# The down product ahead of the next tile's transposes in a routed expert stage

## The reference

```
y = mask * (conv(u * mask, kernel) + u * mask * D)      # (32, 64, 1024)
probs = softmax(y @ gate_w.T)                            # 2048 x 16
w = top 2 of probs, divided by their sum
h = silu(y @ g.T) * (y @ u.T)                            # per expert 112 values
out = x + sum over experts of w * (h @ d.T)
```

## Time and profile before

| | |
|---|---|
| median of 3 runs | 552.07 us (548.31 to 552.22) |
| the profiled execution | 552.11 us, span 550.1 us |
| mean granted TensorE clock | 0.983 |
| TensorE matmuls, weight loads busy | 468.8 us (85%), 404.8 us (74%) |
| VectorE, ScalarE, GpSimd busy | 229.8, 102.7, 182.1 us |
| chain that ended last | TensorE 47%, DMA 32%, VectorE 9%, issue 7% |
| indirect DMAs | 42 gathers, 40 write-backs |
| expert stage, first product to last write-back issued | 268.2 to 540.0 us |

### The profile page before, as it was taken

How to read it: one execution, slowest core, us unless ns; L and a number is a source line. 1 busy time by engine, 2 the same in 40 slices (tenths; PEclk the granted TensorE clock), 3 DMA queues, 4 the chain that set the end, 5 groups by cost and what they waited for, 6 DMA issues and landing times.

```text
span 550.1 us, 9315 instructions
## 1 busy us (share of the span) xinstructions
PE 468.8 (85%) x2835; PEld 404.8 (74%) x2836; DVE 229.8 (42%) x613; ACT 102.7 (19%) x184; POOL 182.1 (33%) x215
## 2 busy tenths in 40 slices
PE   0079899998999999978689999899999899999881
PEld 0079799998999999967567767676666666777660
DVE  7987444445455421585322323233323332333321
ACT  2031111111111101120122222222222222222220
POOL 6355213222222200025233344342442543244431
PEclk9999999999999999997899999999999999999996
DMA  8757999999989987210358789889889778967653
GB/s 287 229 178 246 292 324 334 326 294 310 337 278 345 332 297 234 77 39 1 113 119 225 216 234 265 215 174 294 226 202 263 202 211 193 268 121 167 102 85 62
DMA packets 47783, 119.83 MB, mean 218 GB/s; under 512 B 7698, under 2 KB 24210, under 8 KB 47634
## 3 DMA queue, kind: packets, MB, share of 16 engines
q1 hardware_dynamic: 19314, 73.42, 39.0%
q0 software_dynamic: 11808, 37.76, 31.0%
q10 hardware_dynamic: 16640, 8.39, 5.3%
HBM read 94.62 MB, written 38.57 MB: 242 GB/s over the span
## 4 chain that ended last, share of the span: by engine, by line
PE 47%; DMA 32%; DVE 9%; issue 7%; POOL 3%; POOLq 1%; ACT 0%; DVEq 0%; SPq 0%; ACTq 0%
PE conv_ps L975 22%; DMA out<-od,to_row 16%; DMA ys<-y_rows,from_row 9%; PE conv_ps L1071 9%; PE conv_ps L1089 5%; PE turn_ps L1008 5%; DMA arena<-k_rows 4%; PE turn_ps L1079 3%; DMA k_rows<-k_sb 3%; PE conv_ps L1057 2%; DVE tmp L630 1%; DVE angle L680 1%; POOL out L458 1%; DVE od L920 1%; PE k_bank L967 1%
## 5 line engine op out<-in xcount | busy, mean ns | idle before, releaser
L975 PE MATMUL conv_ps<-arena 128*128 128x256 f32 (+7 forms) x1024 | 150.1, 307 | 6.6 <-DMA arena<-k_rows 5.9
L975 PEld LDWEIGHTS conv_ps<-arena 128*128 128x128 f32 x1024 | 145.3, 191 | 10.8 <-issue 7.0
L1071 PE MATMUL conv_ps<-w_gu,ys_t 128*128 x656 | 136.2, 361 | 13.8 <-issue 11.1
L1071 PEld LDWEIGHTS conv_ps<-w_gu,ys_t 128*128 128x128 f32 x656 | 122.1, 192 | 34.1 <-issue 33.8
L458 POOL DMA_INDIRECT out<-od,to_row x40 | 63.5, 1588 | 133.0 <-DMA out<-od,to_row 85.7
L1089 PE MATMUL conv_ps<-w_d,hid_t 112*128 x160 | 76.2, 598 | 0.0
L442 POOL DMA_INDIRECT ys<-y_rows,from_row x42 | 44.6, 1061 | 45.6 <-PE turn_ps L1079 31.3
L920 DVE TENSOR_SCALAR od<-conv_ps,weight_now 128x512 f32<-128x512 f32 x40 | 30.0, 751 | 70.3 <-DMA out<-od,to_row 47.4
L1079 PE MATMUL turn_ps<-ident,ys 128*128 128x128 f32 x336 | 44.3, 275 | 12.3 <-DMA ys<-y_rows,from_row 12.3
L1079 PEld LDWEIGHTS turn_ps<-ident,ys 128*128 128x128 f32 x336 | 38.2, 141 | 18.2 <-DMA ys<-y_rows,from_row 16.9
L900 DVE TENSOR_TENSOR hid<-silu,conv_ps 128x112 f32<-128x112 f32 x41 | 11.1, 272 | 92.5 <-ACT silu L569 92.4
(11 more groups left out here) (154 smaller groups left out, 328.5 us busy)
## 6 DMA issues: line engine op xcount, KB each, us to landing
arena<-k_rows SPq DMA_DIRECT2D x14, 2048.0 KB, 9.6
w_gu<-gu_t SPq DMA_DIRECT2D x16, 896.0 KB
arena<-x_time SPq DMA_DIRECT2D x16, 512.0 KB, 5.3
y_rows<-y_tok ACTq DMA_DIRECT2D x16, 512.0 KB, 8.9
w_d<-d_t SPq DMA_DIRECT2D x16, 448.0 KB
arena<-k_rows SPq DMA_DIRECT2D x8, 512.0 KB, 6.8
ys<-y_rows,from_row POOLq DMA_INDIRECT x42
out<-od,to_row POOLq DMA_INDIRECT x40
```

The lines of the kernel that those rows point to most:

```text
L975: last = nc.tensor.matmul(conv_ps[:, h, d * B:C * B], toep[:, p, h, d * P:(d + 1) * P], u_t[:, p, h, 0:(C - d) * B], start=(d == 0), stop= ...
L1071: last = nc.tensor.matmul(gu_ps, ys_t[:, p, c, :], w_gu[:, bass.ds(buf * (C * GU) + c * GU, GU)], start=(c == 0), stop=(c == C - 1))
```

## The change

In each step of the expert stage TensorE issues `down(t-1)` ahead of `turn(t+1)`, and no longer behind it. ScalarE issues `weigh_half(t-1)` ahead of `turn_half(t+1)`, and VectorE `weigh_rest(t-1)` ahead of `turn_rest(t+1)`. The same is done in the steps written singly at the start and at the end. GpSimd's and SyncE's queues, all operations, buffers and waits stay the same.

```diff
 # TensorE; ScalarE and VectorE likewise, and the same in the single steps
             gate_up(1, 1)
+            down(0, 0, True)
             turn(2, 0, 1)
-            down(0, 0, True)
             turn_hidden(1, 1)
...
             def pair(i):
                 for p in (1, 0):
                     gate_up(2 * i + 2 - p, p)
+                    down(2 * i + 1 - p, 1 - p, False)
                     turn(2 * i + 3 - p, 1 - p, i + 1)
-                    down(2 * i + 1 - p, 1 - p, False)
                     turn_hidden(2 * i + 2 - p, p)
...
 # ScalarE
                     gate(2 * i + 2 - p, p, False)
+                    weigh_half(2 * i + 1 - p, 1 - p, i, False)
                     turn_half(2 * i + 3 - p, 1 - p, False)
-                    weigh_half(2 * i + 1 - p, 1 - p, i, False)
...
 # VectorE
                     hidden(2 * i + 2 - p, p, False)
+                    weigh_rest(2 * i + 1 - p, 1 - p, i, False)
                     turn_rest(2 * i + 3 - p, 1 - p, False)
-                    weigh_rest(2 * i + 1 - p, 1 - p, i, False)
                     hidden_turned(2 * i + 2 - p, p, False)
```

More of the change, by code:

```diff
@@ L582, in _ @@
             gate(1, 1, True)
+            weigh_half(0, 0, 0, True)
             turn_half(2, 0, False)
-            weigh_half(0, 0, 0, True)
             gate(2, 0, False)
+            weigh_half(1, 1, 0, True)
             turn_half(3, 1, False)
-            weigh_half(1, 1, 0, True)
             def pair(i):
@@ L600, in _ @@
                     gate(t, t % 2, False)
+                    weigh_half(t - 1, (t - 1) % 2, (t - 1) // 2, False)
                     if t + 1 < MT:
                         turn_half(t + 1, (t + 1) % 2, False)
-                    weigh_half(t - 1, (t - 1) % 2, (t - 1) // 2, False)
                 weigh_half(MT - 1, (MT - 1) % 2, (MT - 1) // 2, False)
@@ L929, in _ @@
             hidden(1, 1, True)
+            weigh_rest(0, 0, 0, True)
             turn_rest(2, 0, False)
-            weigh_rest(0, 0, 0, True)
             hidden_turned(1, 1, True)
@@ L934, in _ @@
             hidden(2, 0, False)
+            weigh_rest(1, 1, 0, True)
             turn_rest(3, 1, False)
-            weigh_rest(1, 1, 0, True)
             hidden_turned(2, 0, False)
@@ L952, in _ @@
                     hidden(t, t % 2, False)
+                    weigh_rest(t - 1, (t - 1) % 2, (t - 1) // 2, False)
                     if t + 1 < MT:
                         turn_rest(t + 1, (t + 1) % 2, False)
-                    weigh_rest(t - 1, (t - 1) % 2, (t - 1) // 2, False)
                     hidden_turned(t, t % 2, False)
@@ L1102, in _ @@
             gate_up(1, 1)
+            down(0, 0, True)
             turn(2, 0, 1)
-            down(0, 0, True)
             turn_hidden(1, 1)
             gate_up(2, 0)
+            down(1, 1, False)
             turn(3, 1, 1)
-            down(1, 1, False)
             turn_hidden(2, 0)
@@ L1122, in _ @@
                     gate_up(t, t % 2)
+                    down(t - 1, (t - 1) % 2, False)
                     if t + 1 < MT:
                         turn(t + 1, (t + 1) % 2, (t + 1) // 2)
-                    down(t - 1, (t - 1) % 2, False)
                     turn_hidden(t, t % 2)
```

## The result

The changed kernel took 577.16 us (median of 4 runs, 576.62 to 579.09) beside 552.07 for the kernel before. The ratio is 1.048, with a 95% interval of 1.044 to 1.052. The forecast was 569, range 561 to 589, slower with 0.92. The profiled execution has a span of 575.7 us, 25.6 more than before.

The account below looks back on a forecast made before the run. TensorE was taken as the bound in most expert-stage steps, with late transfers adding. 39 x 6.84 = 266.8 plus 8 late gives 274.8 instead of 256.4, +18.4; end -1: +17.4 on 552.11, 569 us, range 561 to 589.

Parts of the forecast that it names:

- The transposes later: Expert-stage step: the gate product waits for the exposed copy of transposed rows; 6.84 us against 5.88 undisturbed, 0.96 more.
- the other end, 0.73: Copy's end to gate product: alternative to 0.25 us, taken from the stage's second product; 19 us more over 39 steps.
- Gathered rows and issue gaps: TensorE's waits in the 39 steps, 9.6 us for gathered rows and 11.1 us of issue, were to go.
- The wait that changes sides: Evictions waiting for write-backs now stand ahead of the copy and hold the gate product: 8 tiles 1.0 us late, 8 us.
- Rival 4: TensorE's clock falls because it stands still about 1 us every step: 66 us more, 635 us; chance 0.02.
- the forecast case: Exposed copy plus late write-backs, today's gaps absorbed: 569 us, own range 562 to 577; chance 0.72.
- Write-backs: GpSimd's queue: a write-back starts 8.0 us into the step, where it was 7.5, despite earlier evictions; no gain.
- The end: Last tile: the down product goes ahead, so the last write-back starts at about 7 us into the step; 1 us saved.
- Waits that stack up, 589 us: Rival: 37.4 us of exposed copy come on top of today's gaps, none absorbed; 589 us, chance 0.18.
- The opposite sign: Rival: the write-back chain sets the step and earlier evictions save 10.6 us; 541 us, chance 0.04.
- no change: Rival: exposed copies fit in TensorE's room and the write-back chain keeps setting 6.57 us a step; 552 us, chance 0.04.

Follow-up runs that it names:

- TensorE's order alone: TensorE's queue in the changed order, ScalarE's and VectorE's as in the kernel before: 565.4 us, ratio 1.028 against the kernel before.
- release by halves: TensorE's changed order, copies first, ScalarE's copy released after four transposes and the gate product on ScalarE's half: 547.21 us, 0.992 of the kernel before.
- the fillers: Changed kernel plus products of ones behind each hidden transpose: 8 behind the register loads, 601.06 us; 4 ahead of them, 575.48 us.
- order of the evictions alone: ScalarE's and VectorE's queues in the changed order, TensorE's as in the kernel before: 589.25 us, ratio 1.073 against the kernel before.
- filler of 4: Changed kernel plus 4 products of ones directly behind each hidden transpose, ahead of the register loads: 575.48 us, ratio 1.043 against the kernel before.

## Why the prediction was right, point by point

- **The transposes later.** The step was put at 6.84 us and is 6.86. The choice of 0.25 us between copy and product, from the first tile, was right; the other end, 0.73, does not occur in a usual step, but in ten of the longer ones the product starts 0.4 to 0.9 us behind the copy. The run with TensorE's order alone shows this term by itself.
- **Gathered rows and issue gaps.** Both were to go, and they did. Some issue remains, those 2.9 us, where I had put zero.
- **The wait that changes sides.** 8 us were forecast and 8.0 came, but by another way. I had eight write-backs of third tiles, 1 us late each. There were five late ones, up to 2.3 us. In the chain of waits below, a write-back lands after 9.22 us, the next starts 0.91 us later, as one does that enters a new expert, and takes 9.74. It is the second of these for which the eviction at 323.71 waited. The other four are alike: the write-back waited for (started at 298.84, 351.57, 389.26, 462.37) had itself waited for the landing of an earlier one. The prediction had such a pair fit in two steps. That the sum fits is luck.

```profile
303.82 9.22 DMA out<-od,to_row
313.18 0.78 issue
313.95 9.74 DMA out<-od,to_row
```

- **The clock.** Rival 4 was priced as all or nothing, 66 us with 0.02, and left out of the sum. It happened in four steps, 6.5 us. The argument against it looked at gaps of 1.5 us, but the forecast itself had evictions that wait longer than usual on top of a standstill of 1 us in every step. This is the term of the sum that was missing, most of the 8 us between 569 and 577; issue adds 2.9, the step 0.8 (39 x 0.02), and the two ends give 1.8 more back than forecast. 577 is also the upper edge of the forecast case's own range, which was reached by doubling the late evictions and not by the clock. The Trainium skill, "TensorE: Matmul & The Clock Gate", section "HAM oscillation — how this bites in real kernels", says that TensorE falls back to the low clock when it waits for transfers again and again; the trace agrees behind the four longest standstills (2.2 to 3.1 us) and not behind the many of 0.9 to 1.6 us.
- **Write-backs.** "No gain" held, and so did the start at 8.0 us into the step: those of the steps from 437.03 and 443.89 start at 445.07 and 451.94. Over the stage GpSimd's wait for landings went down (85.7 to 51.0 us), its wait for the transposes that the gather needs went up (31.3 to 131.8 us): it has slack now, and TensorE does not gain by it.
- **The end.** 1 us saved was forecast, 1.4 came.
- **Rivals.** Waits that stack up, 589 us: no, the gaps of before were absorbed. The opposite sign and no change: no. (Weight loads were busy for 71% of the stage before and 67% after, and TensorE had no room for the copy all the same.) Something of the opposite sign is in the release by halves: with the copy hidden better, this order is faster than before by 0.8%.

## What to carry to other kernels

Ask of each block on the busiest engine what it hides, and put the longest block that needs nothing new behind the block whose result has to be copied; here 1.7 us of down product stood between the transposes and their copy's use, and moving it left 1.0 us of copy uncovered in every step. In an engine's queue, keep work that may wait for a DMA behind work on which the busiest engine waits. If such an order is wanted for another reason, release the copy in pieces, and price a long standstill twice, for itself and for the lower clock behind it.

## What the runs showed of the hardware that was not expected

- A product of two 128 x 128 fp32 matrices takes about 0.24 us in two matmul records at the full clock (the fillers: 8 in 1.87 us), a transpose of the same size 0.11 us in one (8 start within 0.88 us).
- TensorE's clock did not fall in 39 steps with standstills of 1.5 to 1.6 us each (mean 1.00 over 294.9 us, order of the evictions alone), and fell behind single ones of 1.9 to 3.1 us (changed kernel, filler of 4), at 1.4 to 1.7 us for the gate product that follows. Behind one of 1.74 us it did not.
- A write-back of the same size takes very different times to land: 9.0 and 11.7 us in the earlier trace rows, 9.2 and 9.7 in the chain above, but 5.1 us for the one at 461.25 of the kernel before and 5.8 for the one at 403.87 of the changed kernel. What spreads them was not tried.
